# A four-layer cross-attention decoder on one core: shorter TensorE jobs around the scores, two heads per query projection, wide router operations

## The reference

```python
qh = (q @ Wq).reshape(B, N, NUM_HEADS, HEAD_DIM)      # 16 heads
kh = (kv @ Wk).reshape(B, M, NUM_HEADS, HEAD_DIM)
vh = (kv @ Wv).reshape(B, M, NUM_HEADS, HEAD_DIM)
attn = softmax(einsum('bhnd,bhmd->bhnm', qh, kh) * scale)
out = einsum('bhnm,bhmd->bhnd', attn, vh).reshape(B, N, INNER) @ Wo + bo
```

## Time and profile before

| | before |
|---|---|
| median of 3 runs | 4762.01 us (4760.22 to 4763.99) |
| the profiled execution | 4755.22 us |
| its span, first to last instruction | 4753.4 us |
| mean granted TensorE clock | 0.934 |
| PE busy | 4342.1 us, 91% |
| DVE busy | 3795.6 us, 80% |
| ACT busy | 2388.4 us, 50% |
| POOL busy | 2326.1 us, 49% |

### The profile page before, as it was taken

One profiled execution on the slowest core, in us unless ns is written; L12 is line 12 of the kernel. 1 busy time (PEld: TensorE's weight loads), 2 busy tenths in 40 slices (PEclk: granted clock), 3 DMA queues, 4 the chain that ended last, 5 costly groups with the idle time before them and its releaser, 6 DMA issues.

```text
span 4753.4 us, 100749 instructions
## 1 busy us (share of the span) xinstructions
PE 4342.1 (91%) x41305; PEld 2966.9 (62%) x41305; DVE 3795.6 (80%) x5499; ACT 2388.4 (50%) x4536; POOL 2326.1 (49%) x2453
## 2 busy tenths in 40 slices
PE   6999999879997999999789999996996899999967
PEld 3666666656554666667546766764664566666754
DVE  5888888757777999999779998996555899989842
ACT  3666666523433555555445555552442455555511
POOL 3887888727773454554425555453002254545520
PEclk7999999979997999999789999996997899999975
DMA  3222222013331111111001111110001011111000
GB/s 94 77 83 78 81 82 82 27 47 113 118 100 49 42 35 42 39 37 42 19 26 39 37 42 34 42 36 16 3 1 34 25 36 41 39 37 42 28 11 8
DMA packets 77864, 221.58 MB, mean 47 GB/s; under 512 B 8732, under 2 KB 14124, under 8 KB 76028
## 3 DMA queue, kind: packets, MB, share of 16 engines
q1 hardware_dynamic: 77404, 215.15, 15.2%
HBM read 158.72 MB, written 50.26 MB: 44 GB/s over the span
## 4 chain that ended last, share of the span: by engine, by line
PE 73%; DVE 13%; POOL 7%; ACT 4%; issue 2%; DMA 0%; SPq 0%; POOLq 0%; ACTq 0%; DVEq 0%
PE ps L158 70%; DVE wst L596 4%; POOL wst L383 2%; DVE wst L616 2%; POOL cx L370 2%; POOL cx L377 1%; PE ps L493 1%; DVE xn L147 1%; ACT wst L557 1%; ACT wst L564 1%; DVE st L138 1%; ACT cx L535 1%; PE ps L210 1%; PE ps L197 1%; DVE big L973 1%
## 5 line engine op out<-in xcount | busy, mean ns | idle before, releaser
L564 ACT ACTIVATE wst<-ps 125x448 f32<-125x448 f32 x3072 | 1506.0, 543 | 1212.3 <-PE ps L158 1208.9
L383 POOL TENSOR_TENSOR wst<-wst 125x256 bf16<-125x256 f32 x1536 | 1148.7, 748 | 1392.5 <-ACT wst L564 1346.8
L596 DVE TENSOR_REDUCE wst<-ps 128x2 f32<-128x1000 f32 (+1 forms) x1408 | 1616.5, 1148 | 251.3 <-PE ps L158 248.3
L158 PE MATMUL ps<-big,cx 128*125 128x448 bf16 (+1 forms) x6144 | 1484.8, 360 | 0.0
L616 DVE TENSOR_TENSOR wst<-wst 125x640 bf16<-125x640 f32 x1536 | 1403.5, 914 | 61.5 <-ACT wst L564 60.2
L158 PEld LDWEIGHTS ps<-cx,wst 125*128 125x128 bf16 x23040 | 1138.2, 98 | 381.4 <-issue 52.6
L158 PE MATMUL ps<-cx,wst 125*128 125x65 bf16 (+3 forms) x23040 | 1240.2, 204 | 30.0 <-POOL wst L383 20.8
L158 PE MATMUL ps<-cx,big 128*128 128x500 bf16 (+1 forms) x3584 | 859.2, 337 | 115.5 <-DVE wst L596 97.0
L158 PEld LDWEIGHTS ps<-big,cx 128*125 128x125 bf16 (+1 forms) x6144 | 725.9, 137 | 302.1 <-issue 84.9
L158 PEld LDWEIGHTS ps<-cx,big 128*128 128x128 bf16 x3584 | 225.9, 97 | 486.4 <-DVE wst L596 378.7
L158 PE MATMUL ps<-xT,wa 128*128 128x448 f32 x640 | 301.8, 586 | 1.2 <-ACT wb L255 0.8
(11 more groups left out here) (197 smaller groups left out, 3890.2 us busy)
## 6 DMA issues: line engine op xcount, KB each, us to landing
cx<-ctxN SPq DMA_DIRECT2D x64, 377.9 KB
cTs<-in_ctxT SPq DMA_DIRECT2D x64, 375.0 KB, 5.0
cx<-in_ctxN SPq DMA_DIRECT2D x64, 375.0 KB
cx<-ctxT SPq DMA_DIRECT2D x64, 375.0 KB, 3.7
ctxN<-cx SPq DMA_DIRECT2D x32, 377.9 KB
ynN<-cx SPq DMA_DIRECT2D x32, 377.9 KB
cx<-ynN SPq DMA_DIRECT2D x32, 377.9 KB
ctxT<-cx SPq DMA_DIRECT2D x32, 375.0 KB, 6.7
```

What stands on the lines that cost most here:

```text
L158: return t.matmul(o, l, r, start=start, stop=stop, skip_group_check=True)
L383: g.tensor_tensor(pl[r][0:KP, at:], pf[r][0:KP, at:], pf[r][0:KP, at:].bitcast(BF16)[:, 1::2], ALU.subtract).then_inc(s["plp"], 1)
L564: e.activation(pf[T % 3][0:KP, cols], bank(2 + n2 % 3, 448)[0:KP], ACT.Exp, scale=scale).then_inc(s["ev"], 1)
L596: v.tensor_reduce(o, of, AX.X, ALU.max).then_inc(s["red"], 1)
```

## The change: five edits

1. **Maxima rows.** `top` is made two steps earlier (12k - 5). At 12k - 4 one product turns all of it to 7x128, ACT copies it to `topT` (7x128 bf16), and SP sends that by a DMA to row 64 of `Ql` (`sp_shift`); the scores of batch k wait for the transfer (`wait_shift`).
2. **Query projections** take two heads a product (`wa2`, 8 products a chunk). ACT and DVE still split head by head, 64 rows x 448 columns each, in two successive steps. Each head's `Qh` lands in one half of the rows only; two DMAs a chunk (`sp_double`) copy it to the other, and the first maxima wait for them. At the start of a stage they are two for batch 0 and two for batches 1 to 7.
3. **First maxima of batch 0** alternate between banks 0, 1 and banks 2, 3 (`pair_bank`).
4. **The accumulator** begins at column 2620, so the cut group has 65 and 64 columns.
5. **Routers.** The bias is added by DVE, in the instruction that reads the product, instead of by PE, and `dve_rank` handles all 16 token groups in five instructions, with its 0/1 results in bf16.

```diff
-                if (k := due(T, -2)) >= 0:
-                    for j0, j1 in ((0, 4), (4, NJ)):
-...
-                        for j in range(j0, j1):
-                            r = mm(t, bank(2 + n2 % 3)[64:65, 128 * (j - j0):128 * (j - j0) + 128], top[k % 2][:, j:j + 1], idb[:, :],
-                                   True, True)
+                if (k := due(T, -4)) >= 0:
+                    w.wait_ge(s["nmx"], b0 + k + 1)
+                    if n2 >= 3:
+                        w.wait_ge(s["ev"], evac + n2 - 2)
+                    mm(t, bank(2 + n2 % 3, 128)[0:NJ], top[k % 2][:, :], idb[:, :], True, True).then_inc(s["rw"], 1)
+                    n2 += 1
...
-                        w.wait_ge(s["ev"], evaced_rows(ci, k))
+                        wait_shift(w, ci, k)
                         mm(t, o, chx[k % 2][:, keys], Ql[0:65, k % HB, cols], False, True).then_inc(s["sc"], 1)
...
+        def sp_shift(y, w, ci, k):
+            w.wait_ge(s["ev"], (2 * NT + B) * ci + 2 * max(0, KT * k - 4) + k + 1)
+            y.dma_start(Ql[64:65, k % HB, :], topT[k % 2][:, :]).then_inc(s[f"tops_{k % 2}"], 16)
...
+        def sp_double(y, w, ci, c, first, last):
+...
+            w.wait_ge(s["pa"], 64 * ci + 16 * (c + 1))
+            y.dma_start(Qh[64:128, o, 0:HQ // 2], Qh[0:64, o, 0:HQ // 2]).then_inc(sm, 16)
+            y.dma_start(Qh[0:64, o, HQ // 2:], Qh[64:128, o, HQ // 2:]).then_inc(sm, 16)
...
             if i < 12:
-                return ("project", "split")[i % 2] if p < 12 and p % 4 < 3 and h < H else "", c + 1, h
+                return ("project", "split 0", "split 1", "")[i % 4] if p < 12 and p % 4 < 3 and g < H // 2 else "", c + 1, g
...
-                if k or u:
+                wait_doubled(w, ci, k)
...
+                if k:
                     w.wait_ge(s["red"], q)
+                elif u >= 2:
+                    w.wait_ge(s["red"], q - 1)
...
-                    r = mm(t, bank(n % 2, 500), Qh[:, k % HB, 128 * j:128 * j + 128], cs[k % 3][:, 500 * c:500 * c + 500],
+                    r = mm(t, bank(pair_bank(k, u) + n % 2, 500), Qh[:, k % HB, 128 * j:128 * j + 128], cs[k % 3][:, 500 * c:500 * c + 500],
...
-                        at = 2560 + 129 * j
+                        at = 2620 + 129 * j
...
-                    mm(t, bank(7, 448), wav[:, k, :], tok8(qsrc, p), True, True).then_inc(s["pm"], 1)
-                    split += 1
+                    mm(t, bank(7, 448), wa2[:, k, :], tok8(qsrc, p), True, True).then_inc(s["pm"], 1)
+                    split += 2
...
-            for p in range(nb):
-                v.tensor_tensor(g1[:, p], vj[:, p], vi[:, p], ALU.is_ge).then_inc(sm, 1)
-...
+            v.tensor_tensor(g1, vj, vi, ALU.is_ge).then_inc(sm, 1)
+            v.tensor_tensor(g2, vj, vi, ALU.is_gt).then_inc(sm, 1)
...
-                mm(t, o, xT[:, 128 * p:128 * p + 128], gw, True, False)
-                r = mm(t, o, one[0:1, :], crow[0:1, 0:E], False, True)
+                r = mm(t, o, xT[:, 128 * p:128 * p + 128], gw, True, True)
```

More of the change, by code:

```diff
@@ L93, in build @@
         top = [sb(f"top{i}", [128, NJ], BF16) for i in range(2)]
+        topT = [sb(f"topT{i}", [NJ, 128], BF16) for i in range(2)]
         rden = [sb(f"rden{i}", [128, NJ]) for i in range(2)]
@@ L214, in build @@
         EARLY = (1, 2)
[L215 to L216 removed]
+        FOLD_A = (1, 3, 5, 7, 8)
+        FOLD_D = (1, 1, 1, 3, 4)
         FOLD_HI = (8, 24, 40, 44, 52)
@@ L230, in dve_fold @@
                 w.wait_ge(s["f1"], jobs1[f] + j + 1)
-                for d in range(copies):
-                    v.tensor_copy(fold_out(n)[:, per * j:per * j + per, d, :],
-                                  bank(4 + j).rearrange("p (h c) -> p h c", c=n)).then_inc(s["f1d"], 1)
+                v.tensor_copy(fold_out(n)[:, per * j:per * j + per, :],
+                              bank(4 + j).rearrange("p (h c) -> p h c", c=n)).then_inc(s["f1d"], 1)
             for j in range(4):
@@ L245, in act_fold @@
                 w.wait_ge(s["f1"], jobs1[f] + j + 1)
-                for d in range(copies):
-                    e.activation(fold_out(n)[:, per * j:per * j + per, d, :],
-                                 bank(4 + j).rearrange("p (h c) -> p h c", c=n), ACT.Copy).then_inc(s["f1a"], 1)
+                e.activation(fold_out(n)[:, per * j:per * j + per, :],
+                             bank(4 + j).rearrange("p (h c) -> p h c", c=n), ACT.Copy).then_inc(s["f1a"], 1)
             for j in range(4):
@@ L302, in sp_cross_split @@
                 u = k % 2
+                if k == 2:
+                    sp_double(y, w, 0, 0, 0, 1)
+                    sp_double(y, w, 0, 0, 1, 8)
+                if k > 8 and k % 8 == 1 and k < B:
+                    sp_double(y, w, 0, k // 8, 0, 8)
                 if (j := k - 3) >= 0:
```

168 lines of the change are left out of this document (91 added, 77 removed), and 2 rows, old and new, of the table s.

## The result

The changed kernel takes 4692.36 us (median of 4 runs, 4688.03 to 4694.96) against 4761.11 us (4757.01 to 4763.99) before: a ratio of 0.9855 with a 95% interval of 0.9838 to 0.9872, so 69 us or 1.45% faster. The forecast was 4589, with a range from 4500 to 4680. The time lies 12 us above that range and 103 us above the forecast, and of the 173 us that it had counted on, 69 came.

What follows compares the result with a forecast made beforehand. The prediction saw the ring between PE and DVE, PE's work and DVE's work in balance. Its terms, -58 - 18 - 14 - 42 - 5 - 36 = -173, took 4762 to 4589 us, range 4500 to 4680 (8 in 10).

Steps and rivals of the forecast that it cites:

- so .72 is lost: Loops, slot T = 22 of 24: removing the maxima-row wait saves .72 us for each of 64 batches, 46 us.
- T = 10: Loop slot of the other 64 batches: no DVE wait, products cost almost nothing, .1 us taken each, 6 us in sum.
- -18: Loops, query projections: a product's visible share is .19 us a head, 37 us over 192 heads; half the products go.
- end of +24: Loops, slow end for projections: back-to-back splits may cost up to .25 us more for each of 96 pairs.
- the 2.5 that the forecast had named: Loops, a sign to check: steps with two splits in a row should stay under 2.5 us.
- The accumulator: -14 forecast: Loops, value products: the uneven cut costs at most .04 us a step, counted for 383 maxima that waited for PE.
- First maxima: -42 forecast: Batch 0 of each stage: with two bank pairs only a .03 us handshake remains, -10.4 us a stage.
- Stage starts: -5 forecast: Start of a stage: ACT's splits end 3.6 us earlier, then DMA issues and landing; ends -12 and +11.
- Routers: -36 forecast: Routers of layers 0 and 3: bias products save 8.3 and 8.6 us, ranks 8.9 and 9.7; ends -30 and -42.
- The ring of 1.89: Plain loop step: DVE reads banks, PE refills them, DVE reads again; this sets 1.89 us between maxima.
- The first rival: The loops gain nothing because DVE is the limit; only first maxima, starts and routers gain, -83: 4679 us, chance .20.
- the unchanged pace without projections: Loop steps without projections, a sign: staying at 2.0 us means ring or DVE bounds it; below 1.9, PE did.

Runs made afterwards that it cites:

- a1: The kernel before with only the maxima rows changed (one transpose and a DMA): 4734.5 us, loops 3266.6 against 3263.2.
- b1: The changed kernel with the second split of each two-head product one step later: loops 3240.5 us against 3280.7 in the changed kernel.
- a4: The changed kernel with the query projections put back to one head a product and splits every other step: 4635.7 us, loops 3255.0.
- c4: c1 with the remainder cut to 512 columns on DVE and 384 on POOL, before 640 and 256: loops 3168.3 us.
- a2: The kernel before with only the query projections changed (two heads a product, splits in successive steps, doubling by DMA): 4729.6 us, loops 3270.2.
- a3: The kernel before with only the accumulator moved to column 2620: 4718.6 us, loops 3248.5.
- c1: The changed kernel with splits spaced, POOL's last operation for a batch two steps later and its cast on ACT one step later: 4595.8 us.

## Why the prediction was wrong, and where it was right

**The step that failed: maxima rows.** The forecast took the 2.61 us between two maxima, a plain step of 1.89, "so .72 is lost", and counted 58 us with what stood beside it. The wait was there and it went. Alone the edit changed the loops by +3.4 us (a1), of which +3.9 in the first stage, where the new transfer was late, and -0.5 in the other three. What the step left out is that DVE's wait was cover for POOL's operation on the same kind of data. In the crossed runs the edit is worth +3.4 with that operation in its old place and -40.1 with it moved. The profile before had the sign in it: its remainders take 914 ns in the mean where an undisturbed one takes .81 us, and at T = 10 the maxima stood 2.24 apart with no wait of DVE for PE between them, .35 more than in a plain step; the remainder between them took 1.21, behind POOL's operation. I read that only as "DVE is held by its own work".

The Trainium skill states the rule, and I had not weighed it: page "SBUF — State Buffer", section "Who interferes with whom", says that a DVE instruction with two SBUF inputs contends with a GpSimd instruction that reads SBUF, that what they share is an exclusive lock, and that the order of issue decides who blocks, while `tensor_reduce` never contends on this chip. The traces agree: 1.24 in place of .81 with .55 of overlap, 1.54 with an operation that began .15 earlier and lasted 1.01, POOL's 1.01 grown to 1.48 where the remainder was first, and the maximum at 1.18 to 1.20 throughout. By that rule the gain of edit 1 would have been judged by where POOL stands when the wait goes.

**The term that was mis-sized: projections.** The forecast took -18 and named "two splits in steps that follow each other" as an end of +24. The edit as made measured +7.0 alone and +25.6 with the others; with the splits spaced, -27.4 alone and -14.6 with the others (b1 against a4). So the direction of the -18 was right for half the products, its size near the smaller of the two, and the end of +24 was the truth for the splits (25.6 with the other edits). It should have been part of the sum, since the order of the instructions showed two splits in a row. Of the steps that hold such splits (1, 2, 5, 6, 9 and 10) all but one stayed under the 2.5 that the forecast had named; step 9 takes 2.55 in the changed kernel.

**Right.** The accumulator: -14 forecast, -14.7 measured, by its own reasoning (PE is late in some steps), but both factors were off and made up for each other. From the first value product to the product behind the values it went from .639 to .617 us, so .022 a step and not .04 (near the 23 ns that the forecast had estimated for the short product), and the gain is what 43% of the 1536 steps would give, not 383 of them. First maxima: -42 forecast, -44.4. Stage starts: -5 forecast, -6.3. The copies for batch 0 landed 2.0 us after their issue in the median, not 2.6; this agrees with the 2.0 that the forecast had set beside its sum, though the section that it named is about transfers issued by GpSimd, and SP issued these. Routers: -36 forecast; -17.0 between the first two stages and 10.2 + 10.9 in layer 3 make -38. Here luck helped: five operations at the forecast's own price come to 22, not 21, and the `max` in bf16 gave 2.1 back. The ring of 1.89 in the plain step held under c4. The first rival (the loops gain nothing, 4679) came nearest to the time, and the unchanged pace without projections speaks for it; but its reason, that the steps close up against DVE, lacks the collision with POOL, which made them longer.

**Not seen.** The transfers of the maxima in the first stage: ahead of its first remainder +4.6 us, of which 3.98 are the wait for the first one, which landed after 11.9 us, and 4.5 more inside its loop. In a4, in which 13 were waited for inside it, that loop got 3.6 longer and the other three 3.4 to 4.4 shorter, so the late transfers may cost some 8 us there. The forecast had read 2.6 and 6.7 us as the fastest and the slowest landing, but they are medians, of transfers of 187.5 and 375 KB. And the clock after the last loop: -30.1 there, 21.1 for the router and 8 to 9 by the clock. That part of the gain is luck; a1, a2 and a3 got about 30 us by it for nothing.

Summed from single edits (a1, a2, a3) the loops would be 4.3 us shorter; together they are 17.5 longer. Of these 21.8, 3.1 come from joining the rows and the accumulator (-8.2 in a4, where the single edits give -11.3), and 18.6 from the projections, which cost 25.6 there and 7.0 alone. Why they cost more beside the other edits was not taken apart.

## What to carry to other kernels

When a wait of a full engine is removed, look at what ran on other engines under it, and above all at operations that get longer beside each other: the wait may have been the time in which the neighbour ran at no cost. Ask then which of the two will begin first, since here the one that began second got longer. Judge such an edit by crossed runs (the edit with and without the neighbour moved), and by stretches of the trace that hold only its code. A total that moves by 30 us with an edit that touches nothing in the stretch that moved is no measurement of the edit. A DMA put into a loop should be looked at in every stage: here it was late only in the first.

## What the runs showed of the hardware that I had not expected

- A DVE operation on two tiles in on-chip memory that starts .15 us after a POOL operation of 1.01 us takes 1.54 us in place of .81. If the DVE operation starts .21 us before it, DVE's keeps .82 and POOL's takes 1.48. DVE's reductions from PSUM keep 1.18 to 1.20 us beside the same POOL operations.
- The same 240 products behind the ranks of layer 3 took 66.5 us at a mean granted clock of 0.94 in one kernel (a4) and 97.8 us at 0.59 in another (b1, PE busy 88.6 of them); the same kernel (c1) ran in 4574 and in 4620 us.
- A transfer of 1.8 KB between tiles, issued behind eleven large ones, released its waiter after 11.9 us, and took SP .84 us to issue; five later ones that were waited for in the same stage took 8.4 to 9.0.
